# A graph layer's edge sort: bucket tables on partitions, and the sort product with its operands swapped

## The reference

```
xn  = layernorm(x)
agg = segment_sum(xn[dst] * edge_weight[:, None], src, num_segments=6250)
h   = relu((xn + agg) @ W1 + b1) @ W2 + b2
x   = x + h + linear_attention(xn)
out = x + mixture_of_16_experts_top_2(layernorm(x))
```

## Time and profile before

| | us |
|---|---|
| median of 3 runs | 2087.97 (2083.77 to 2088.9) |
| the profiled execution's own time | 2086.33 |
| its span, first to last instruction | 2084.2 |
| PE busy | 1814.0 (87%) |
| DVE busy | 1411.1 (68%) |
| POOL busy | 1206.1 (58%) |
| ACT busy | 741.2 (36%) |

### The profile page before, as it was taken

The page is one execution under the profiler, slowest core; times in us unless marked ns, Lnnn a source line. Parts: engine busy times, 40 slices in busy tenths (PEclk is TensorE's granted clock), DMA queues, the critical chain, the costliest instruction groups (busy, mean ns, idle before and its releaser), DMA issues. The chain is left out here.

```text
span 2084.2 us, 43884 instructions
## 1 busy us (share of the span) xinstructions
PE 1814.0 (87%) x12300; PEld 1634.0 (78%) x12300; DVE 1411.1 (68%) x4015; ACT 741.2 (36%) x2167; POOL 1206.1 (58%) x1244
## 2 busy tenths in 40 slices
PE   6306999758889999999999999999977999999986
PEld 4206889657878888888888888878766999999974
DVE  5899788758996777677767776657554555555547
ACT  5806778500101333333333332222222333333347
POOL 1003444477777777777777777777703555555424
PEclk9657999979999999999999999999978999999999
DMA  5000101054444444444444444444425642222248
GB/s 174 0 0 21 39 22 39 22 166 149 137 132 120 129 127 129 130 134 129 128 129 128 130 125 125 123 121 128 120 84 163 208 126 72 72 72 72 69 148 316
DMA packets 130018, 232.33 MB, mean 111 GB/s; under 512 B 25990, under 2 KB 82616, under 8 KB 129703
## 3 DMA queue, kind: packets, MB, share of 16 engines
q0 software_dynamic: 56096, 144.39, 23.8%
q1 hardware_dynamic: 46039, 59.76, 8.8%
q10 hardware_dynamic: 27696, 25.83, 3.9%
HBM read 187.46 MB, written 42.43 MB: 110 GB/s over the span
## 5 line engine op out<-in xcount | busy, mean ns | idle before, releaser
L1337 POOL DMA_INDIRECT lower<-xn_rows,lower x858 | 826.9, 964 | 261.5 <-issue 232.8
L1502 DVE TENSOR_SCALAR lower<-bank,lower 128x128 f32<-128x128 f32 x960 | 347.1, 404 | 69.6 <-issue 53.1
L1362 PE MATMUL bank<-ones,ident 128*128 128x128 f32 x2376 | 322.5, 278 | 23.3 <-DVE xh L1519 17.8
L1362 PEld LDWEIGHTS bank<-ones,ident 128*128 128x128 f32 x2376 | 307.4, 192 | 40.4 <-DVE xh L1519 20.7
L1378 PE MATMUL bank<-lower 128*128 x960 | 292.2, 386 | 19.9 <-SPq L1207 13.1
L1519 DVE TENSOR_TENSOR xh<-xh,bank 128x256 f32 x480 | 199.3, 415 | 158.4 <-PE bank L1379 156.9
L1379 PE MATMUL bank<-lower 128*128 x960 | 287.3, 380 | 0.0
L608 POOL DMA_INDIRECT edge_records_sorted<-lower x112 | 113.2, 1011 | 292.3 <-ACT lower L771 266.7
L2003 DVE TENSOR_SCALAR arena<-bank,b_tile 128x128 f32<-128x128 f32 x456 | 128.4, 345 | 166.4 <-PE bank L1881 166.4
L1881 PEld LDWEIGHTS bank<-arena 128*128 128x128 f32 x1824 | 224.6, 194 | 14.6 <-ACT arena L1936 8.9
L1881 PE MATMUL bank<-arena 128*128 128x128 f32 x1824 | 225.6, 278 | 8.1 <-ACT arena L1936 8.1
(11 more groups left out here) (347 smaller groups left out, 2594.7 us busy)
## 6 DMA issues: line engine op xcount, KB each, us to landing
lower<-xn_rows,lower POOLq DMA_INDIRECT x858
lower<-in_L_ffn_w SPq DMA_DIRECT2D x16, 512.0 KB
upper<-in_L_ffn_w SPq DMA_DIRECT2D x16, 512.0 KB
xn_rows<-xh SPq DMA_DIRECT2D x7, 896.0 KB, 4.1
lower<-xn_rows ACTq DMA_DIRECT2D x49, 128.0 KB
xn_rows<-lower ACTq DMA_DIRECT2D x49, 128.0 KB
x_plus_beta<-lower ACTq DMA_DIRECT2D x49, 128.0 KB
upper<-in_x SPq DMA_DIRECT2D x1, 6144.0 KB
```

What stands on the lines that cost most here:

```text
L1337: pool.indirect_dma_start(edge_rows[:, t % ROUND, :], None, xn_dram, bass.IndirectOffsetOnAxis(source.bitcast(U32)[:, t:t + 1], 0)).then_i ...
L1362: pe.matmul(sums_at(u)[:, 0:P], ident[:], ones[:], start=True, stop=True)
L1502: dve.tensor_scalar(edge_sel[:, (2 * u + h) % ESEL, :], iota_gather, lane[:, at:at + 1], weight_s[:, at:at + 1], ALU.is_equal, ALU.mult).t ...
```

## The change

Four things change together.

1. The counts are taken after d = 2, 4, ..., 14, not 3, 7, ..., 27. The prefix matrix `upto_b` is now exclusive, with its first column set to one, so that row 0 of `cnt` holds the totals and the other rows the edges above.
2. SP sends row 0 of `cnt` to 49 partitions (`totals`), one bucket on each. The tables are then 49 x 28 on DVE, with small products in between for first quads, keys, ranks, bases, the order of the buckets and the steps. These products stand inside PE's loop over d (`sums(16)`, `sums(17)`, `sums(19)`, `sums(21)`), so that PE waits there for SP and DVE. The 56 products of L683 and the three wide operations of `bucket_order` go.
3. In the sort loop the step matrices are bf16 on 114 partitions, and the sort product has its operands swapped: the weights are `row_hot`, 128 x 128, the moving operand is the payload, 128 x 64. The result comes out upright, so that one copy by ACT remains, and the transpose goes.
4. The ranks of the experts go to another bank of PSUM, which moves their unit numbers by -2 to +2; the last unit stays 498.

```diff
+            sp.wait_ge(s_cnt, NR)
+            sp.dma_start(totals[0:NT, :], cnt[0:1, :]).then_inc(s_totals, 16)
...
+            def sums(d):
+                if d == 16:
...
+                    pe.wait_ge(s_small, 1)
+                    pe.matmul(first_at, before[0:NT, 0:NT + 1], quads_b[0:NT, :], start=True, stop=True).then_inc(s_pref, 1)
+                if d == 17:
+                    pe.wait_ge(s_small, 2)
+                    pe.matmul(keys_at, key_wide[0:NT, :], ident[0:NT, 0:NT], start=True, stop=True).then_inc(s_pref, 1)
+                    pe.wait_ge(s_small, 3)
+                    for c, (b0, nb) in enumerate(BANKS):
+                        pe.matmul(bank[2 * c][:, 0:nb * NGRP], ones[0:NT, :], spread[0:NT, b0 * NGRP:(b0 + nb) * NGRP],
+                                  start=True, stop=True).then_inc(s_pref, 1)
+                if d == 19:
+                    pe.wait_ge(s_small, 4)
+                    pe.matmul(bases_at, ahead[0:NT, :], total_one[0:NT, :], start=True, stop=True).then_inc(s_pref, 1)
+                if d == 21:
+                    pe.wait_ge(s_small, 5)
+                    pe.matmul(sorted_at, key_wide[0:NT, :], placed_at[0:NT, :], start=True, stop=True).then_inc(s_pref, 1)
+                    pe.matmul(steps_at, one_less[0:NT + 1, 0:NT + 1], due_b[0:NT + 1, :], start=True, stop=True).then_inc(s_pref, 1)
...
-                if d % 4 == 3:
-                    count(d // 4)
...
+                if d % 2 == 0 and d <= 2 * NR:
+                    count(d // 2 - 1)
+                sums(d)
...
                 for c in range(NQ):
-                    mm = pe.matmul(bank[2 + p][:, c:c + 1], past_m[p][0:NT + 1, c * P:(c + 1) * P], ones[0:NT + 1, 0:1],
+                    mm = pe.matmul(bank[2 + p][:, c:c + 1], past_m[p][0:KB, c * P:(c + 1) * P], steps_b[0:KB, ds(g, 1)],
                                    start=True, stop=True)
...
                 for e in range(GC):
-                    mm = pe.matmul(bank[6 + p][0:NQ * QW, 0:P], moving[p][:, e].rearrange("p c w -> p (c w)"),
-                                   row_hot[p][:, e, :], start=e == 0, stop=e == GC - 1)
+                    mm = pe.matmul(bank[6 + p][:, 0:NQ * QW], row_hot[p][:, e, :], moving[p][:, e].rearrange("p c w -> p (c w)"),
+                                   start=e == 0, stop=e == GC - 1)
                 mm.then_inc(s_qmm, 1)
-                pe.wait_ge(s_qx, g + 1)
-                pe.sem_inc(s_apart, 1)
-                pe.transpose(bank[1][:, p * P:p * P + NQ * QW], quads_across,
-                             ident[0:NQ * QW, 0:NQ * QW]).then_inc(s_qT, 1)
...
-                act.activation(quads_across, bank[6 + p][0:NQ * QW, 0:P], ACT.Copy).then_inc(s_qx, 1)
-                act.wait_ge(s_qT, g + 1)
...
-                act.activation(quads[i], bank[1][:, p * P:p * P + NQ * QW], ACT.Copy).then_inc(s_qcp, 1)
+                act.activation(quads[i], bank[6 + p][:, 0:NQ * QW], ACT.Copy).then_inc(s_qcp, 1)
```

```diff
+            dve.wait_ge(s_totals, 16)
+            then(dve.tensor_scalar(totals_i[kb, :], totals[kb, :], float(QE - 1), None, ALU.add))
+            then(dve.tensor_scalar(totals_i[kb, :], totals_i[kb, :], QSHIFT, None, ALU.arith_shift_right))
+            dve.tensor_copy(quads_b[kb, :], totals_i[kb, :]).then_inc(s_small, 1)
...
+            dve.tensor_tensor(bg(spread)[kb], ident[kb, 0:NT].unsqueeze(2).to_broadcast([NT, NT, NGRP]),
+                              bucket_fq8[kb, :].unsqueeze(1).to_broadcast([NT, NT, NGRP]), ALU.mult).then_inc(s_small, 1)
...
+                dve.wait_ge(s_pref, 3 + c)
+                dve.scalar_tensor_tensor(start[:, at], cnt[:, at], not_first, bank[2 * c][:, 0:nb * NGRP], ALU.mult, ALU.add).then_inc(s_dve, 1)
...
+            dve.wait_ge(s_pref, 3 + len(BANKS))
+            then(dve.tensor_copy(total_one[kb, :], bases_at))
+            then(dve.tensor_scalar(due_b[kb, :], upto_g[kb, :], total_one[kb, 0:1], None, ALU.add))
+            dve.tensor_scalar(placed_at[kb, :], iota_n[kb, 0:NT], total_one[kb, 1:2], None, ALU.is_equal).then_inc(s_small, 1)
```

More of the change, by code:

```diff
@@ L208, in gps_layer @@
         cnt = carve(NBG)
[L209 to L212, removed]
-        NR = NT // GT
[L215 to L223, removed]
+        look_at = EC + NBG
+        second_match = carve(4 * (EC // 2) + 3 * EC)
+        match_words = carve(GT * EC // 2)
+        match = [a.bitcast(BF16)[:, 0:GT * EC] for a in (match_words, second_match)]
+        assert GT * EC // 2 <= 4 * (EC // 2) + 3 * EC
+        NR = NT // GT
+        assert GT * NGRP <= 512 and NR % 2 == 1
+        spread = carve(NBG)
+        totals, bucket_fq8, due_b, quads_b, upto_g = (carve(NGRP) for _ in range(5))
+        totals_i = carve(NGRP).bitcast(I32)
+        key_col, rank_col, base_col, not_first = (carve(1) for _ in range(4))
+        total_one = carve(2)
+        key_wide, one_less = carve(P), carve(P)
+        ahead, placed_at = carve(NT), carve(NT)
+        carve = carver(xh[:, sort_at + look_at:NT * D], NT * D - sort_at - look_at)
         masks = [carve(EC // 2).bitcast(U16) for _ in range(4)]
@@ L322, in gps_layer @@
         kvs = carve(DC * P)
-        base, bucket_key, bucket_rank, bucket_of = (kvt[:, k * NT:(k + 1) * NT] for k in range(4))
+        base, bucket_of = (kvt[:, k * NT:(k + 1) * NT] for k in range(2))
         kvm_flat = kvm.rearrange("p c e -> p (c e)")
@@ L586, in edges_gpsimd @@
             pool.memset(shift_down, 0.0).then_inc(s_poolc, 1)
-            pool.memset(last_row, 0.0).then_inc(s_poolc, 1)
-            pool.wait_ge(s_poolc, 4)
+            pool.wait_ge(s_poolc, 3)
             pool.affine_select(out=shift_down, in_=shift_down, compare_op=ALU.not_equal, fill=1.0, base=1,
                                pattern=[[-1, P]], channel_multiplier=1).then_inc(s_consts, 1)
[L591 to L600, removed]
             def scatter(r, i):
@@ L665, in edges_tensor @@
                     differences(d + 2)
-                if d % 4 == 3:
-                    count(d // 4)
[L668 to L684, removed]
+                if d % 2 == 0 and d <= 2 * NR:
+                    count(d // 2 - 1)
+                sums(d)
+            assert 2 * NR < 16 and 16 * NGRP >= EH
             def sort(r, i):
@@ L793, in edges_vector @@
             n = dve_n
+            high, low = slice(0, NT + 1), slice(LOW, KB)
             dve.memset(src_i, 0).then_inc(s_clear, 1)
@@ L832, in edges_vector, with then @@
                     dve.tensor_copy(cnt[:, (r - 1) * GT * NGRP:r * GT * NGRP], bank[(r - 1) % 2][:, 0:GT * NGRP]).then_inc(s_cnt, 1)
-            dve.wait_ge(s_pref, 2 * len(BANKS))
+            def then(ins):
+                ins.then_inc(s_dve, 1)
+                dve.wait_ge(s_dve, n.add())
+            kb = slice(0, NT)
+            dve.tensor_copy(due_b[0:KB, :], aside[0:KB, :]).then_inc(s_dve, 1)
+            dve.memset(total_one, 1.0).then_inc(s_dve, 1)
+            dve.memset(bucket_quads[:, NT:NT + 1], 0.0).then_inc(s_dve, 1)
@@ new lines, in edges_vector @@
+            dve.tensor_copy(quads_b[kb, :], totals_i[kb, :]).then_inc(s_small, 1)
+            dve.wait_ge(s_small, 1)
+            then(dve.tensor_tensor_scan(upto_g[kb, :], ones[kb, 0:NGRP], quads_b[kb, :], 0.0, ALU.mult, ALU.add))
+            dve.tensor_copy(total_one[kb, 0:1], upto_g[kb, NGRP - 1:NGRP]).then_inc(s_dve, 1)
+            n.add()
+            then(dve.scalar_tensor_tensor(key_col[kb, :], upto_g[kb, NGRP - 1:NGRP], 64.0, iota_pc[kb, 0:1], ALU.mult, ALU.add))
+            dve.tensor_copy(key_wide[kb, :], key_col[kb, :].to_broadcast([NT, P])).then_inc(s_small, 1)
@@ new lines, in edges_vector @@
+            dve.wait_ge(s_pref, 1)
+            dve.tensor_scalar(bucket_fq8[kb, :], first_at[kb, :], float(QE), None, ALU.mult).then_inc(s_dve, 1)
+            dve.tensor_copy(first_col[high, :], first_at).then_inc(s_dve, 1)
+            dve.tensor_copy(first_col[low, :], first_at).then_inc(s_dve, 1)
+            dve.wait_ge(s_dve, n.add(3))
+            dve.tensor_tensor(bg(spread)[kb], ident[kb, 0:NT].unsqueeze(2).to_broadcast([NT, NT, NGRP]),
+                              bucket_fq8[kb, :].unsqueeze(1).to_broadcast([NT, NT, NGRP]), ALU.mult).then_inc(s_small, 1)
@@ L838, in edges_vector @@
             dve.wait_ge(s_dve, n.add(len(BANKS)))
[L839 to L846, removed]
@@ L1154, in gps_layer @@
             u = max(turn_unit[s] + 15, rank_unit[-1] + 2 if s else 0)
-            while any(u + d - T_SECOND in turn_unit for d in (-1, 0, 1)):
+            while u in turn_unit or u - 1 in turn_unit:
                 u += 1
```

126 lines of the change are left out of this document (47 added, 79 removed).

## The result

The changed kernel takes 2162.52 us (median of 4 runs, 2157.89 to 2166.95), the kernel before 2088.39 beside it (4 runs). The ratio is 1.036, 95% interval 1.0334 to 1.0386: slower by 3.6%. The profiled execution has a span of 2160.8 us, 76.6 more than the earlier trace rows.

A forecast was written before the change was run, and what follows sets the result against it. Stages add up: DVE bounds tables and lookups, PE paces the sort loop, PE and POOL share the edge phase. -38.6 + 0.8 + (350 - 237.0) - 0.65 = +74.6 on 2086.3 gives 2161 us, range 2125 to 2195.

The forecast's parts named there:

- step c: Sort loop: PE's clock stays at 0.50 through all 28 turns and a turn lasts 12.4 us; chance 0.80.
- A pass: Sort loop: one swapped product with its weight load costs 0.213 us at the low clock, 0.108 to 0.110 at the high.
- The loop's size: Sort loop: 28 x (11.95 + 0.43 + 0.02), plus 0.4 us at six round ends, together 350 us, before 237.0.
- The tables (a, b): Before the sort loop: last count's copy ends near 42.6, lookups start near 55, 38.6 us earlier, and end near 117.
- Waits of DVE (d): Sort loop: DVE waits for PE some 6 us a turn.
- After the loop (e, f): Edge phase: first gather of L1337 issued at about 426 + 75 = 501, stages from there as long as before.
- the ranks' move: Edge phase: ranks move by at most two units, new waits are for things done two or more units earlier: 0.
- Rival 1: Sort loop: clock rises in the first turns and stays, DVE bounds at 6.6 us a turn: 1999 us; chance 0.13.
- Rival 2: Sort loop: clock rises for part, each high turn saves 5.8 of 12.4 us: 1999 to 2161; 0.07 with Rival 4.
- Rival 3: Tables: wait in `sums` or transfer takes 20 us, lookups begin at 70: 2176 us with low clock; chance 0.03.
- Rival 4: Only the tables gain, sort loop unchanged: 2086 - 38 = 2048 us; chance 0.07 together with Rival 2.

The follow-up runs named there:

- j_bridge: Changed kernel, moving columns read twice in the first four sort-loop turns, four extra 64-column products behind each turn's: 2030.88 us against 2087.48 for the kernel before, 0.972.
- l_swap_only: Kernel before with only the sort product's operands swapped, without second copy, transposition and wait; old tables, counts, placing products, ranks: 2238.11 us against 2087.48, 1.0713.
- b_warm: Changed kernel with 14 filling products of 128 float32 columns ahead of the sort loop's first turn: 2461.31 us, 1.0267 of the kernel before.
- i_kick: Changed kernel with the moving columns read twice (128 for 64) in the sort loop's first four turns only: 2436.19 us against 2399.4 for the kernel before, 1.0148.
- c_wide: Changed kernel with each sort product's 64 moving columns read twice, in the whole loop: 2317.98 us against 2397.32 for the kernel before, 0.9665.
- a_oldprod: Changed kernel with the sort product's old operands, copy across and transposition put back; tables, counts, ranks as changed: 2343.37 us against 2397.32 for the kernel before, 0.9792.
- after_again: The changed kernel unaltered, on a chip where the kernel before takes 2399.4 us: 2460.75 us, ratio 1.0272.

## Why the prediction was right, and where its terms were off

**The clock (step c): shown.** The step that carried the forecast was that the products with 128 weights and 64 columns would not raise the clock. Undoing the swap takes the loss away, the swap alone makes it, and doubling the columns, which asks more of PE, gives 141 us of loop back. The weighing of the earlier trace rows was the right one: PE busy with loads is not PE busy with columns. The Trainium skill, "TensorE: Matmul & The Clock Gate", part 1 (The HAM clock gate), has sustained activity release the throttle; here PE was busy for 339.8 of 351 us and stayed at 0.50, so the trace doesn't bear out that plain reading. One row was given more weight than it bears: the 5.3 us from 207.6 on are of L700's products with 128 columns, the same that raised the clock in the first turn. They show only that the rise took its time, while the row at 93.6, of one-column products, does stand for loads.

**A pass: right.** 12.13 us less 0.15 of placing, over 56 passes, is 0.214; the prediction took 0.213 from L692.

**The loop's size: 10.2 us too much.** 350 was forecast and 339.8 measured. The placing products cost 0.15 in a turn and not 0.43, since the next products begin before their last one ends, which is 7.8 over 28 turns; the six gaps of 0.4 at the ends of rounds aren't there, 2.4.

**The tables (a, b): right within 1.4 us.** The last count's copy ended at 43.40 (42.6), DVE had the totals at 45.72 (45.0), the lookups began at 56.28 (55.0). The first product came at 132.09, forecast 130.7.

**Waits of DVE (d): right in kind**, 5.4 us a turn for some 6.

**After the loop (e, f): one term priced at nothing is there.** The first gather is at 491.9; 501 was forecast, and the 9 us are the loop's 10.2 less the tables' 1.4. From there the stages were to be as long as before, and they are 10.8 us longer. The sentence that failed is the one that gives the ranks' move a cost of 0. PE's waits from 515 us on in the changed kernel (us in total, times, longest):

```profile
PE bank L1375 <- ACT lower L1236: 15.6, 17, 1.2
```

L1375 is the rank product. Its result now lies in bank 3, where `turn` writes as well, and so it waits for `s_hTe`, ACT's copy of the turned rows. "Done two or more units earlier" was wrong for 17 of 49. j_bridge has the same row to the digit, though its phase begins 133 us earlier:

```profile
PE bank L1379 <- ACT lower L1240: 15.6, 17, 1.2
```

l_swap_only's list has no such row, nor has the list of the kernel before. From the first gather to the end it is 1658.1 us in the kernel before and 1658.4 in l_swap_only, with the old ranks, and 1668.9 in the changed kernel and 1669.9 in j_bridge, with the new ones, wherever the phase begins (at 426.1, 577.1, 491.9 and 358.5). In the code behind the loop only the ranks are edited. So their move comes to 10.5 to 11.8 us where PE is the bound, and little is left to chance in where the phase stands. What is missing is this edit undone alone on such a chip.

How 15.6 us of waits, 14.8 of them between the first and the last unit, become 11 can be read from PE's other waits. The first two lines are of the changed kernel from 515 to 1600 us, the third of the kernel before from 440 to 1540:

```profile
PE bank L1421 <- ACT lower L1254: 8.3, 7, 2.0
PE bank L1351 <- SPq L1180: 1.9, 2, 1.0
...
PE bank L1378 <- SPq L1207: 13.1, 13, 2.5
```

The gate's product (L1421), which nobody edited, now waits for another copy by ACT, and PE, being later, waits 11.2 us less for gathered rows. From the first to the last unit PE's waits come to 51.1 us before and 63.1 after. Why ACT's copy for the gate comes late isn't shown.

The total of 2161 against 2162.5 is thus partly luck: -10.2 of the loop, +1.4 of the tables and +10.8 of the edge phase offset each other. A small reading was off without any effect: the gathers of the kernel before stood 0.30 us apart ((1087.2 - 826.9) / 858) and not 0.27.

**The rivals.** Rival 1 (the clock rises and stays) was described with a false condition: "it decides as soon as PE gets out of the low level once". In b_warm and i_kick PE was at the high level at the loop's entry and in its fifth turn, and lost it both times. Its 1999 us was low as well: with the clock high, c_wide's loop is 198.6 us and not 188, a turn 7.1 and not 6.6, because ACT's payload half (L745) is also waited for, 13 us in 12 waits. Rival 2 is what i_kick was made into: five turns at the high level for 24.6 us, 4.9 each where the prediction gave 5.8, since the first begins low and DVE and ACT set the pace of the others. Rival 3 is out: from the last copy's end to DVE's first operation on the totals it is 2.3 us. Rival 4's old product with new tables is a_oldprod: 54 us gained where 38 were given, since its loop is 217.7 us and not the unchanged 237.0.

## What to carry to other kernels

Before operands are swapped, look at how many columns stream behind each load of weights, and at what clock the nearest rows of that mix ran: here one swap that removes a transpose, a wait and a copy from each turn cost 151 us. Where a loop's clock stays low with PE never idle, try more moving columns, even useless ones, before less work; behind 128 float32 weights the second 64 were free here (6.44 and 6.50 us a group). Where few columns must stay few, close the pauses: that kept the level in j_bridge, for 1.06 us a turn. And give a price to every new wait in a phase that PE bounds, even if what it waits for seems long done.

## What the runs showed of the hardware that was not expected

- The same products held the clock or lost it, and what differed were their pauses: with 64 columns behind 128 weights it stayed at 1.00 for 24 turns without a pause (j_bridge), and was lost after one pause of 0.81 us (i_kick) and one of 2.09 us (b_warm). With 128 columns (c_wide) pauses of up to 1.4 us did nothing; the one of 5.36 us in the kernel before (weights of 64 columns) did, for the clock is at 0.50 behind it. At the low level 28 turns of 64 columns without a pause didn't raise it.
- The same program took longer on three chips: the gathers of the edge phase lasted 1365 to 1383 us there against 1087 to 1092, the kernel before 2379 to 2399 us against 2088, and the change cost 2.7% (2399 us) and not 3.6% (2088 us). The gathers' packets took no longer: queue q0 is at 22.7% of 16 engines' 2160.8 us in the changed kernel, 490 us, and at 20.2% of 2451.3 us, 495 us, in after_again. POOL's instruction for a gather took 966 and 961 ns. What took longer isn't shown. Nor is it shown that the chip itself is the reason, since each of the three was measured at one time only.
